# Layer 1's experts: row tiles turned by VectorE from quartered loads, in place of TensorE

## What is computed

```python
E, G, TKG, K = (32, 8, 4, 8)
I, SI = (256, 512)
x = hidden_states.reshape(-1, H)                  # 2048 x 512
...
_, top_k_index = jax.lax.top_k(masked, K)
tkw = jnp.take_along_axis(scores, top_k_index, axis=-1)
...
flat_idx = top_k_index.reshape(-1)
sort_idx = jnp.argsort(flat_idx)
xs = jnp.repeat(x, K, axis=0)[sort_idx]           # rows in the order of their experts
group_sizes = jnp.bincount(flat_idx, length=E).astype(jnp.int32)
gate = jax.lax.ragged_dot(xs, w_gate, group_sizes)
up = jax.lax.ragged_dot(xs, w_up, group_sizes)
down = jax.lax.ragged_dot(jax.nn.silu(gate) * up, w_down, group_sizes)
routed = (down[unsort].reshape(T, K, H) * tkw[..., None]).sum(axis=1)
```

## Time and profile before

| what | us |
|---|---|
| median of 3 runs | 3164.42 |
| the profiled execution | 3160.61 |
| its span, first to last instruction | 3158.9 |
| TensorE busy (matmuls) | 2766.6 (88%) |
| TensorE weight loads | 1261.3 (40%) |
| VectorE busy | 1432.9 (45%) |
| ScalarE busy | 773.7 (24%) |
| GpSimd busy | 1367.9 (43%) |
| mean granted TensorE clock | 0.951 |

### The profile page before, as it was taken

How to read it: one execution, slowest core, us unless ns; L and a number is a source line. 1 busy time by engine, 2 the same in 40 slices (tenths; PEclk the granted TensorE clock), 3 DMA queues, 4 the chain that set the end, 5 groups by cost and what they waited for, 6 DMA issues and landing times. The chain is left out here.

```text
span 3158.9 us, 34747 instructions
## 1 busy us (share of the span) xinstructions
PE 2766.6 (88%) x9571; PEld 1261.3 (40%) x9572; DVE 1432.9 (45%) x2766; ACT 773.7 (24%) x1190; POOL 1367.9 (43%) x960
## 2 busy tenths in 40 slices
PE   5888975899999887689999989942999999999998
PEld 2343431344444333233333334411555555555454
DVE  7999999422000231366566646200333333333332
ACT  4746643200000010234433421000111111111111
POOL 2777656033000221165645322553555555455554
PEclk8998999899999998889999989975999999999999
DMA  3333221211201699730671013443766666776654
GB/s 123 117 102 101 80 66 48 111 54 34 92 13 44 226 355 322 204 96 1 186 196 51 1 39 130 168 162 136 162 142 150 142 121 130 187 153 150 130 91 71
DMA packets 303703, 386.00 MB, mean 122 GB/s; under 512 B 51058, under 2 KB 208307, under 8 KB 303602
## 3 DMA queue, kind: packets, MB, share of 16 engines
q1 hardware_dynamic: 212434, 243.23, 24.4%
q0 software_dynamic: 68272, 97.19, 15.6%
q10 hardware_dynamic: 22896, 44.30, 5.2%
HBM read 237.10 MB, written 160.27 MB: 126 GB/s over the span
## 5 line engine op out<-in xcount | busy, mean ns | idle before, releaser
L1856 POOL DMA_INDIRECT out_x<-e_yo,e_dest x318 | 493.4, 1552 | 467.7 <-DMA out_x<-e_yo,e_dest 243.1
L1991 PE MATMUL e_psg<-e_wgu,e_xsT 128*128 x1272 | 583.2, 601 | 2.9 <-SPq L1827 1.9
L285 POOL TENSOR_TENSOR hc<-hs,bcst 128x1024 f32<-128x1024 f32 x128 | 301.5, 2356 | 177.1 <-DVE ps_b L505 169.9
L1991 PEld LDWEIGHTS e_psg<-e_wgu,e_xsT 128*128 128x128 f32 x1272 | 230.0, 191 | 237.6 <-issue 235.7
L630 PE MATMUL ps_y<-hc,ident 128*128 128x512 f32 x512 | 243.5, 614 | 89.2 <-POOL hc L285 88.9
L2007 PE MATMUL e_pso<-e_wd,e_hT 128*128 x636 | 299.0, 592 | 0.7 <-DVE e_hT L1932 0.7
L1937 DVE TENSOR_TENSOR e_h<-e_psg,e_sg 128x256 f32<-128x256 f32 x159 | 67.6, 425 | 504.9 <-ACT e_sg L1877 486.2
L511 DVE TENSOR_TENSOR_SCAN hs<-dA,ps_b 128x1024 f32<-128x1024 f32 x128 | 292.7, 2286 | 6.8 <-ACT dA L415 2.6
L1877 ACT ACTIVATE e_sg<-e_psg 128x256 f32<-128x256 f32 x159 | 61.1, 384 | 676.3 <-PE e_psg L1991 676.3
L1230 PE MATMUL r_ps_t<-r_wd,r_h 128*128 128x512 f32 x480 | 211.1, 601 | 10.4 <-issue 5.3
L877 POOL DMA_INDIRECT slots_in<-r_xn,scat x128 | 126.6, 989 | 169.8 <-DMA slots_in<-r_xn,scat 98.3
(11 more groups left out here) (415 smaller groups left out, 3786.0 us busy)
## 6 DMA issues: line engine op xcount, KB each, us to landing
e_xs<-slots_in ACTq DMA_DIRECT2D x159, 272.0 KB
slots_in<-zeros SPq DMA_DIRECT2D x160, 256.0 KB, 2.3
bcst<-bc_rows SPq DMA_DIRECT2D x128, 256.0 KB, 4.2
e_wgu<-in_wg SPq DMA_DIRECT2D x32, 512.0 KB
e_wgu<-in_wu SPq DMA_DIRECT2D x32, 512.0 KB
e_wd<-in_wd SPq DMA_DIRECT2D x32, 512.0 KB
e_w<-in_wg SPq DMA_DIRECT2D x11, 1408.0 KB
e_w<-in_wu SPq DMA_DIRECT2D x11, 1408.0 KB
```

What stands on the lines that cost most here:

```text
L285: pool.tensor_tensor(hc[:, it % 2, half(h), :], hs[:, it % 2, half(h), :], bc(bcst[:, q, 1, :], 1, HB), ALU.mult).then_inc(sem["hc"], 1)
L1856: pool.indirect_dma_start(halves, bass.IndirectOffsetOnAxis(dest[:, q, a:a + 1], 0), yo[:, q, a * HC:(a + 1) * HC], None, bounds_check=2 * ...
L1991: j = pe.matmul(ps_g[:, q % 2, :], xsT[:, q % 2, k, :], wgu[:, bass.ds(e % RING, 1), k, :], start=k == 0, stop=k == KH - 1)
```

## The change

Loads now go by pairs of tiles, 256 rows, into one of two buffers. Four DMAs bring the row's columns in quarters: quarter a (128 columns) of row s*32 + j goes to partition a*32 + j, place s. A fifth brings the 17 words of each record to a tile of its own, `rec`. VectorE then turns a tile in one instruction, in blocks of 32x32 within each group of 32 partitions, and that gives the same `xsT` as before. TensorE's row transposes, their PSUM tile and the semaphore `tr` are gone. The loads are issued behind `empty`, every second tile. The wait for the loaded rows moves from TensorE to VectorE.

```diff
-        xs = pl.sb("e1_xs", [P, RING, XW])
+        PAIRS = NSLOT1 // (2 * P)
+        DQ = 32
+        NQ = P // DQ
+        RECW = 2 * K1 + 1
+        xs = pl.sb("e1_xs", [P, 2, 2 * NQ, P])
+        rec = pl.sb("e1_rec", [P, 2, 2, XW - H])
...
-        ps_x = pl.ps("e1_psx", [P, 2, 512])
...
-        rows_in = [pl.sem0(f"e1_rows{q}") for q in range(RING)]
+        rows_in = [pl.sem0(f"e1_rows{r}") for r in range(2)]
...
-                def load(t, q):
-                    act.dma_start(xs[:, q % RING, :], D["xs1"][bass.ds(t * P, P), :]).then_inc(rows_in[q % RING], 16)
+                def load(row0, r):
+                    for a in range(NQ):
+                        act.dma_start(xs[a * DQ:(a + 1) * DQ, r, :, :],
+                                      D["xs1"][bass.ds(row0, 2 * P), a * P:(a + 1) * P].rearrange("(s j) c -> j s c", j=DQ))\
+                           .then_inc(rows_in[r], 16)
+                    act.dma_start(rec[:, r, :, 0:RECW], D["xs1"][bass.ds(row0, 2 * P), H:H + RECW]
+                                  .rearrange("(u p) w -> p u w", p=P)).then_inc(rows_in[r], 16)
 
                 def reload(t, q):
-                    hold(act, sem["tr"], 1 + t + 1, c["held"])
+                    hold(act, sem["xsT"], 1 + t + 1, c["held"])
                     hold(act, sem["dest"], 1 + t + 1, c["held"])
-                    load(t + RING, q)
+                    load((t + 3) * P, q // 2 % 2)
...
                 with act.Fori(2, TURNS - 1) as i:
                     for q in range(OUT):
                         gate(i * OUT + q, q)
-                        reload(i * OUT + q - 1, q + OUT - 1)
                         empty(i * OUT + q - 1, q + OUT - 1)
+                        if q % 2 == 0:
+                            reload(i * OUT + q - 1, q + OUT - 1)
...
-                def turned_rows(t, q):
-                    dve.wait_ge(sem["tr"], 1 + t + 1)
-                    dve.wait_ge(sem["gu"], 1 + t - 1)
-                    dve.tensor_copy(xsT[:, q % 2, :, :], ps_x[:, q % 2, :].rearrange("p (k s) -> p k s", s=P))\
-                       .then_inc(sem["xsT"], 1)
+                def turned_rows(t, q, n, first=False):
+                    if q % 2 == 0:
+                        dve.wait_ge(rows_in[q // 2 % 2], 16 * (NQ + 1) * n)
+                    if not first:
+                        dve.wait_ge(sem["gu"], 1 + t - 1)
+                    four = slice(q % 2 * NQ, (q % 2 + 1) * NQ)
+                    dve.transpose(xsT[:, q % 2, :, :].rearrange("p k (s j) -> p k s j", j=DQ),
+                                  xs[:, q // 2 % 2, four, :].rearrange("p s (i k) -> p k s i", k=KH)).then_inc(sem["xsT"], 1)
...
                 def addressed(t, q):
-                    row = xs[:, q % RING, :]
+                    row = rec[:, q // 2 % 2, q % 2, :]
...
-                def turn_rows(q, landed_count):
-                    pe.wait_ge(rows_in[q % RING], landed_count)
-                    for k in range(KH):
-                        j = pe.transpose(ps_x[:, q % 2, k * P:(k + 1) * P], xs[:, q % RING, k:H:KH], c["ident"][:, :])
-                    j.then_inc(sem["tr"], 1)
...
-                        if not (last and q == LAST - 1):
-                            pe.wait_ge(sem["xsT"], 1 + t)
-                            turn_rows(q + 1, 16 * (i + 1 + (q + 1) // RING))
```

More of the change, by code:

```diff
@@ L1885, in empty @@
                        .then_inc(sem["yo"], 1)
-                def load(t, q):
-                    act.dma_start(xs[:, q % RING, :], D["xs1"][bass.ds(t * P, P), :]).then_inc(rows_in[q % RING], 16)
+                def load(row0, r):
[5 more added lines that the diff above has]
+                                  .rearrange("(u p) w -> p u w", p=P)).then_inc(rows_in[r], 16)
                 def reload(t, q):
-                    hold(act, sem["tr"], 1 + t + 1, c["held"])
+                    hold(act, sem["xsT"], 1 + t + 1, c["held"])
                     hold(act, sem["dest"], 1 + t + 1, c["held"])
-                    load(t + RING, q)
-                for q in range(RING):
-                    load(q, q)
+                    load((t + 3) * P, q // 2 % 2)
+                for r in range(2):
+                    load(r * 2 * P, r)
                 for t in range(OUT):
@@ L1899, in _ @@
                     if t > 0:
+                        empty(t - 1, t - 1, first=True)
+                    if t > 0 and t % 2 == 0:
                         reload(t - 1, t - 1)
-                        empty(t - 1, t - 1, first=True)
                 gate(OUT, 0)
+                empty(OUT - 1, OUT - 1, first=True)
                 reload(OUT - 1, OUT - 1)
-                empty(OUT - 1, OUT - 1, first=True)
                 for q in range(1, OUT):
                     gate(OUT + q, q)
-                    reload(OUT + q - 1, q - 1)
                     empty(OUT + q - 1, q - 1)
+                    if q % 2 == 0:
+                        reload(OUT + q - 1, q - 1)
                 with act.Fori(2, TURNS - 1) as i:
@@ L1916, in _ @@
                     gate(t, q)
-                    if t - 1 + RING < NTILE1:
+                    empty(t - 1, q + OUT - 1)
+                    if q % 2 == 0 and t // 2 + 1 < PAIRS:
                         reload(t - 1, q + OUT - 1)
-                    empty(t - 1, q + OUT - 1)
                 empty(NTILE1 - 1, REST - 1)
@@ L1943, in addressed @@
                         dve.wait_ge(sem["added"], 1 + t - OUT + 1)
[L1944 to L1946 removed]
+                    dve.scalar_tensor_tensor(out=mine[:, q % 2, :], in0=row[:, K1:2 * K1], scalar=slot1[:, bass.ds(t, 1)],
+                                             in1=row[:, 0:K1], op0=ALU.is_equal, op1=ALU.mult).then_inc(sem["named"], 1)
+                    dve.scalar_tensor_tensor(out=pad[:, q % 2, :], in0=row[:, 2 * K1:RECW], scalar=0.0, in1=spare1[:, :],
                                              op0=ALU.is_equal, op1=ALU.mult).then_inc(sem["named"], 1)
@@ L1949, in addressed @@
                     dve.tensor_reduce(wrow[:, q, :], mine[:, q % 2, :], AX_X, ALU.add).then_inc(sem["chosen"], 1)
-                    dve.scalar_tensor_tensor(out=dest[:, q, 0:1], in0=pad[:, q % 2, :], scalar=-1.0, in1=row[:, H + 2 * K1:H + 2 * K1 + 1],
+                    dve.scalar_tensor_tensor(out=dest[:, q, 0:1], in0=pad[:, q % 2, :], scalar=-1.0, in1=row[:, 2 * K1:RECW],
                                              op0=ALU.add, op1=ALU.add).then_inc(sem["first"], 1)
                     dve.wait_ge(sem["first"], 1 + t + 1)
-                    dve.tensor_tensor(dest[:, q, 1:2], pad[:, q % 2, :], row[:, H + 2 * K1:H + 2 * K1 + 1], ALU.add)\
+                    dve.tensor_tensor(dest[:, q, 1:2], pad[:, q % 2, :], row[:, 2 * K1:RECW], ALU.add)\
                        .then_inc(sem["dest"], 1)
@@ L1969, in _ @@
                 dve.wait_ge(sem["preset"], 1 + 2)
-                dve.wait_ge(sem["tr"], 1 + 1)
-                dve.tensor_copy(xsT[:, 0, :, :], ps_x[:, 0, :].rearrange("p (k s) -> p k s", s=P)).then_inc(sem["xsT"], 1)
+                turned_rows(0, 0, 1, first=True)
                 a_round(0, first=True)
```

6 lines of the change are left out of this document (3 added, 3 removed).

## The result

The changed kernel is slower by 11%. The median of four runs is 3517.44 us (3512.01 to 3518.69), beside 3161.34 for four runs of the kernel before on the same chip: a ratio of 1.1131, with a 95% interval of 1.1116 to 1.1145. The forecast was 3460 in a range of 3320 to 3560. The profiled execution took 3512.01, so 351.4 more than the profiled one before. In the runs further down, early, behind and the kernel before each had one execution far above its others (6063.34, 7251.44 and 4814.76 us), which ratios and intervals leave out and which moves a median by at most 1.5 us.

What follows compares the result with a forecast made beforehand. TensorE's instructions were taken to bound the expert stage, 11.87 us a pair. A load stall (14.01) plus clock fall (1.71) made 15.72, +3.85 over 78 pairs: 3160.6 + 299 = 3460 us, range 3320 to 3560.

Steps and rivals of the forecast that it cites:

- The wait: Expert stage: TensorE idles 3.2 us a pair before the down product, which starts at +8.61 instead of +5.40.
- L: Time from first issue to last landing of a pair's five loads: 3.74 to 4.99 us, taken as 4.9.
- The transpose: VectorE's 128x512 block transpose, taken at the copy's 0.69 us, with 1.14 from the scan in the range.
- the 43 us: Estimate on VectorE: at 1.24 us a transpose, 0.55 us a pair more, some 43 us longer.
- The quartered pieces: Row loads in 512-byte pieces: 2.1 us of all 16 engines a pair, transfer volume unchanged, no new bound.
- 44 us more: Estimate for loads to 32 partitions at 218 GB/s: 0.60 us a piece, 0.56 a pair, sum 44 us higher.
- The clock: Each TensorE stall brings a fall to 1.2 GHz, costing 1.7 us a pair on the products.
- The weights: Rival: 29 weight loads in the stage each delay a row load by 4.6 us, +133, 3593; chance 0.13.
- What goes: Four row transposes a tile leave TensorE: 0.47 us a tile, 73 us if nothing took their place.
- The third rival: In the stage the wait hides and the transposes' time comes back, all 73 us (3087); chance 0.07.
- The sum: A pair takes 15.72 us against 11.87, +3.85; 78 pairs give +300, less 1 before the first stall.

Runs made afterwards that it cites:

- early: The changed kernel with a pair's five loads issued ahead of the emptying of the tile before; 3353.53 us, ratio 1.0626.
- behind: The kernel before with only its row loads moved behind the emptying, still in four buffers; 3164.21 us, ratio 1.0028.
- ring4: The changed kernel with four pair buffers instead of two, each load issued for the pair two pairs later; 3154.12 us, ratio 1.0004.
- fill: The changed kernel with three needless products on TensorE before the down product in every second tile; 3485.41 us, ratio 1.1048.
- hoista: The changed kernel with TensorE's expert read and weight wait moved ahead of its wait for the hidden rows; 3540.42 us, ratio 1.1219.
- wshift: The changed kernel with an expert's weights issued only once rows of three more tiles are turned; 3400.24 us, ratio 1.078.
- hoist4: ring4 with TensorE's expert read and weight wait moved ahead of its wait for the hidden rows; 3112.72 us, ratio 0.9865.
- deep: hoist4 with sixteen output and address buffers instead of eight; 3122.41 us, ratio 0.9889.

## Why the prediction was right, and where not

**The wait, right.** Its place, its chain (load, transpose, copy of hidden rows, down product), its count (79 in the view of waits, 78 forecast) and the issue at +2.36 stand as forecast, and a longer lead alone takes all of it away (ring4). L = 4.9, taken near the upper bound, was 4.89 in the clean pair shown, 4.70 in the mean of 50, and 4.60 in the 32 with a full clock.

**The transpose, mis-sized.** The step that took the copy's 0.69 failed: 1.08, inside its bounds of 0.69 and 1.14 and near the scan's rate. The 0.39 us that this adds to a pair were nearly paid back by the load, 4.60 instead of 4.9, so the 32 clean pairs came to 14.08 instead of 14.01: 5 us in 78 pairs. That is two errors that cancel, and not a sum that was right in both. The Trainium skill (VectorE: DVE Perf Modes, The three transpose paths) has 311 ns for 128x128 in bf16, and four of these gave an estimate of 1.24; the measured 1.08 lies between, nearer to it than the 0.69 taken. As long as the load is early, the duration costs nothing (ring4), so the 43 us worked out from that estimate were no fixed price either.

**The quartered pieces, right.** Transfer time is no bound: from 2200 to 3480 ScalarE's queue held 13.4% of the engines for 41.75 MB, 172 us of all 16, where the earlier trace rows had 16.7% of 959 us, 160, for 43.18 MB. That is 2.2 us a pair, where 2.1 was forecast. The estimate worked out from the Trainium skill (SBUF — State Buffer, Door 1: The DMA port swizzle), at its 218 GB/s for 32 partitions, was 44 us more. No such cost shows: with that term L would have been 5.46, and it came out at 4.70 in the mean; ring4 has the same pieces and the time of the kernel before, though its long lead would hide a slower landing.

**The clock, half wrong.** The step "I charge each with a fall" failed in its count: 43 stretches, about 80 us, where 78 x 1.71 = 133 were charged. Its price by piece, 80 / 43 = 1.85, was near the 1.71. The waits here, 2.67 us in the mean without the long ones, lie where some bring a fall and some do not. The two runs that change the idle time move the count as they should, fill to 17 and hoista to 58. Which waits bring one was not settled.

**The weights, a rival that came true in part.** They were put at up to 133 for 29 sets, chance 0.13, and left out of the sum. To put them at nothing in the sum was the largest single error. Measured: the 28 loads near them took 3.61 longer, 101 us, of which the 15 waits over 6 us (8.5 each beside 2.67 for the others) make 88; wshift gives 113 with the falls that they bring. The price by piece (4.6 from the DMA rate) was below the 5.4 of the row shown and the 6.0 of the 15 in the mean (10.74 - 4.70). That only half of the sets collide comes from loading by pairs: as shown above, a set meets a load when the finished tiles are even in number, 15 times of 28.

**What goes, wrong but without effect on the sum.** "Four transposes a tile on TensorE: 0.47" is worth 0.06 (5.93 to 5.87). In the sum this was hidden, because a pair that waits ends by the load, not by TensorE's work. The third rival rested on it: with a load in good time it promised 3087, and ring4, which is that case, took 3154. The earlier trace rows has a sign of it: the products start at 2605.27, 1.38 behind the end of VectorE's product, and of what TensorE did between them only the hidden transposes (0.24) had to wait for that product. That the queue's own read and wait fill this time is in none of the rows; the lines of L1987, above, and hoist4 show it.

**The sum.** Clean pairs 78 x (14.08 - 11.87) = +172, clock +80, loads near weights 28 x (8.31 - 4.70) = +101: +353, against +351.4 in the profiled execution. The forecast's +299 had 167, 133 and 0. So the clock was charged 53 too much and the weights 101 too little. These errors partly cancelled, and that the forecast came within 57 us, inside its range, is in part luck.

## What to carry to other kernels

Before a load's issue is moved, count its lead in the steady state and hold it against its landing time beside the largest transfer that may come at the same moment: four buffers with the same small pieces cost nothing, two cost 11%. An engine that shows as 100% busy may hide its own queue's register work and waits under instructions that nobody needs just then; look for the time from the last true input to the next true output, since it says what removing the filler would give. And look at what an in-order engine holds up behind a wait: exchanging two instructions on VectorE took 138 of 356 us away with no more memory.

## What was not expected of the hardware

- A block transpose of 128x512 float32 with a strided read took VectorE 1.08 us, where a copy of that size took 0.69.
- TensorE's queue needs about 1.3 us from VectorE's product to the next products when a register read (0.30), its arithmetic and a wait on the read value stand between (ring4). When they are moved ahead it is 0.91 (2602.12 to 2603.03 in hoist4), and there TensorE is busy all the time, with the rest of the down product and the hidden transposes.
- Speeding up TensorE's part where it waits made the kernel 26 us slower, through a granted clock of 0.87 instead of 0.91.
- A load issued 1.9 us earlier landed only 1.2 us earlier (4.70 became 5.40). This stays unexplained.
- In the additions, GpSimd is busy 3.10 us a tile and its pace is 5.66, since it waits for earlier additions to land (304.2 us in deep).
